# The first batch rearranged in a Strassen-type fp32 attention kernel: A's first two tiles first, x's first rows first, Wv split in A's place

## The reference

```python
# x (16, 1024, 512), adj (1024, 1024) of zeros and ones, Wq, Wk, Wv (512, 512), all float32
def _L0_gnn_ref(neuron_states, adjacency, Wq, Wk, Wv):
    q = jnp.einsum('bnd,ed->bne', neuron_states, Wq)
    k = jnp.einsum('bnd,ed->bne', neuron_states, Wk)
    v = jnp.einsum('bnd,ed->bne', neuron_states, Wv)
    rel = jnp.einsum('bnd,bmd->bnm', q, k)
    rel = adjacency.T[None, :, :] * rel
    rel = rel / jnp.linalg.norm(rel, axis=2, keepdims=True)
    return jnp.einsum('bnm,bmd->bnd', rel, v)

x = _layernorm(x + _L0_gnn_ref(x, adj, Wq, Wk, Wv), axis=-1)
```

## Time and profile before

| | us |
|---|---|
| median of 3 runs | 1971.78 (1971.39 to 1971.95) |
| the profiled execution, its own time | 1971.97 |
| its span, first to last instruction | 1970.2 |
| PE busy in the span | 1957.0 (99%) |
| DVE, ACT, POOL busy | 1531.9 (78%), 762.5 (39%), 957.8 (49%) |

### The profile page before, as it was taken

How to read it: one execution, slowest core, us unless ns; L and a number is a source line. 1 busy time by engine, 2 the same in 40 slices (tenths; PEclk the granted TensorE clock), 3 DMA queues, 4 the chain that set the end, 5 groups by cost and what they waited for, 6 DMA issues and landing times.

```text
span 1970.2 us, 28685 instructions
## 1 busy us (share of the span) xinstructions
PE 1957.0 (99%) x9857; PEld 1669.1 (85%) x9857; DVE 1531.9 (78%) x2085; ACT 762.5 (39%) x1288; POOL 957.8 (49%) x639
## 2 busy tenths in 40 slices
PE   8999999999999999999999999999999999999998
PEld 6888888888888888888888888888888888888887
DVE  8796877868778696787968779687796877868775
ACT  5433434335342352423424234342433424335341
POOL 5744536455354553446435374453644536455352
PEclk9999999999999999999999999999999999999999
DMA  5734343344524345343444333443434343344401
GB/s 188 314 134 165 144 167 115 144 154 154 186 92 149 142 157 184 122 151 118 157 175 160 128 139 133 172 153 128 160 128 170 144 155 127 144 154 152 185 26 64
DMA packets 80416, 292.22 MB, mean 148 GB/s; under 512 B 7441, under 2 KB 7441, under 8 KB 76305
## 3 DMA queue, kind: packets, MB, share of 16 engines
q1 hardware_dynamic: 80400, 292.06, 40.2%
HBM read 251.13 MB, written 40.89 MB: 148 GB/s over the span
## 4 chain that ended last, share of the span: by engine, by line
PE 97%; DVE 1%; POOL 1%; DMA 0%; issue 0%; SPq 0%; ACT 0%; POOLq 0%; DVEq 0%
PE banks L422 32%; PE banks L424 32%; PE banks L423 32%; DMA scr<-xT 0%; DVE aw L794 0%; DVE x_lo L755 0%; POOL scr L1063 0%; DVE yv L816 0%; POOL square_sum L1067 0%; POOL squares L1067 0%; SPq L344 0%; POOL scr L1072 0%; SPq L343 0%; POOL res L1075 0%; POOL res L1080 0%
## 5 line engine op out<-in xcount | busy, mean ns | idle before, releaser
L422 PE MATMUL banks<-yv 128*128 128x512 f32 x1024 | 399.8, 390 | 0.0
L424 PE MATMUL banks<-yv 128*128 128x512 f32 x1024 | 398.5, 389 | 0.0
L423 PE MATMUL banks<-yv 128*128 128x512 f32 x1024 | 398.5, 389 | 0.0
L1119 POOL TENSOR_TENSOR square_sum<-square_sum,squares 128x512 f32<-128x512 f32 x224 | 319.9, 1428 | 85.7 <-ACT squares L657 75.1
L422 PE MATMUL banks<-yv,x_hi 128*128 128x512 f32 x896 | 348.7, 389 | 0.5 <-DVE rel L857 0.5
L424 PE MATMUL banks<-yv,x_lo 128*128 128x512 f32 x896 | 348.6, 389 | 0.0
L423 PE MATMUL banks<-yv,x_hi 128*128 128x512 f32 x896 | 348.6, 389 | 0.0
L1136 POOL TENSOR_TENSOR rstd<-var_eps,minus_half 128x1 f32<-128x1 f32 x128 | 144.2, 1127 | 329.3 <-DVE var_eps L968 329.3
L423 PE MATMUL banks<-aw,x_hi 128*128 128x256 f32 x896 | 253.6, 283 | 0.0
L424 PE MATMUL banks<-aw,x_lo 128*128 128x256 f32 x896 | 253.5, 283 | 0.0
L422 PE MATMUL banks<-aw,x_hi 128*128 128x256 f32 x896 | 253.5, 283 | 0.0
(11 more groups left out here) (108 smaller groups left out, 3430.5 us busy)
## 6 DMA issues: line engine op xcount, KB each, us to landing
scr<-adj SPq DMA_DIRECT2D x128, 512.0 KB, 5.8
aw<-w_kept SPq DMA_DIRECT2D x16, 3584.0 KB, 11.1
aw<-a_kept SPq DMA_DIRECT2D x15, 3584.0 KB, 11.0
scr<-xT SPq DMA_DIRECT2D x32, 1024.0 KB, 7.1
res<-x SPq DMA_DIRECT2D x128, 256.0 KB, 2.7
out<-res SPq DMA_DIRECT2D x128, 256.0 KB, 2.0
a_kept<-aw SPq DMA_DIRECT2D x1, 3584.0 KB, 18.2
w_kept<-v_raw SPq DMA_DIRECT2D x3, 512.0 KB, 8.5
```

The costliest lines, as they stand in the source:

```text
L422: pe.matmul(bank_ap, l_hi, r_hi, start=first and i == 0, stop=False, skip_group_check=on)
L423: pe.matmul(bank_ap, l_hi, r_lo, start=False, stop=False, skip_group_check=on)
L424: mm = pe.matmul(bank_ap, l_lo, r_hi, start=False, stop=i == len(pairs) - 1, skip_group_check=on)
L1119: pool.tensor_tensor(square_sum[:, h, :], square_sum[:, h, :], squares[:, n % SQRING, :], ALU.add).then_inc(square_added, 1)
```

## The change

In the first batch:

- PE makes A in another order: k = 0, 1 for all four banks, then k = 2, 3 for banks 0 and 1, then for 2 and 3. The six idle products go.
- x's first half is loaded first; the pieces of x come in the order X11, X22, S1, X12, S2, S3, S4. S1 to S4 are all made on POOL, S1 and S2 into free space of `rel`.
- The pieces of A are ordered B11, T1, B21, T2, T4, B22, between those of x; T3's lo piece moves to POOL with a semaphore of its own.
- The staging of Wv goes: its four sums and seven lo pieces move from POOL to DVE, into the first pair of the first scores; the seven hi copies move on ACT behind the squares of m11. They write straight into `aw` once A has been stored, and the last lo piece sets `w_loaded`. The seven small stores become one of 3.5 MB, the load of Wv in the first batch goes.
- adj row 2 is loaded at the very start.

In every batch S2 stands ahead of S3. Nothing else of batches 1 to 15 changes in kind.

```diff
-X_PIECES = (X22, X11, S1, X12, S3, S2, S4)
-X_SUMS = (S1, S3, S2, S4)
+X_PIECES = (X11, X22, S1, X12, S2, S3, S4)
+X_SUMS = (S1, S2, S3, S4)
...
-        A_PIECES = (B11, T1, B21, T2, T4, T3, B22)
+        A_PIECES = (B11, T1, B21, T2, T4, B22)
...
# SP
-            load_x(0)
+            load_x(0, (0, 1))
...
+            load_adj(2)
             load_adj(3)
...
                 if first:
-                    for i in range(3, 7):
-                        store_wv(i)
-                    load_adj(2)
-                    sp.wait_ge(a_split, 7)
+                    sp.wait_ge(a_split, len(A_PIECES))
+                    sp.wait_ge(a_t3_split, 1)
                     sp.dma_start(a_kept, aw[:, :].bitcast(F32)).then_inc(a_stored, DMA)
+
+                    sp.wait_ge(w_loaded, DMA)
+                    sp.dma_start(w_kept, aw[:, :].bitcast(F32)).then_inc(w_stored, DMA)
                     for t in range(RRING):
                         load_res(0, t)
-                    for i in range(WSLOTS):
-                        sp.wait_ge(w_stored[i], 2 * DMA if i < 3 else DMA)
-                    sp.wait_ge(a_stored, DMA)
-
-                sp.wait_ge(y_done, b * Y_COUNT + Y_COUNT)
-                sp.dma_start(aw[:, :].bitcast(F32), w_kept).then_inc(w_loaded, DMA)
+                else:
+
+                    sp.wait_ge(y_done, b * Y_COUNT + Y_COUNT)
+                    sp.dma_start(aw[:, :].bitcast(F32), w_kept).then_inc(w_loaded, DMA)
                 sp.wait_ge(s_m12, b * HT + 1)
                 load_adj(6)
...
# PE
+            for ks, js in (((0, 1), range(KD)), ((2, 3), (0, 1)), ((2, 3), (2, 3))):
+                for k in ks:
+                    pe.wait_ge(w_split, 2 * k + 2)
+                    for j in js:
...
-            for i in range(FILL_PRODUCTS):
-                pe.matmul(bank[0], zeros[:, 0:P], zeros[:, 0:BANK], start=True, stop=True)
...
# ACT
+                act.wait_ge(a_stored, DMA)
+                act.wait_ge(y_done, Y_COUNT)
+                act.activation(wv_hi[:, q, :, :], wv_raw_of[q], ACT.Copy).then_inc(wv_hi_made, 1)
...
-            for q in (X22, X11, S1):
-                x_piece(0, q, True)
+            x_piece(0, X11, True)
             a_hi_piece(B11)
             act.activation(a12_raw, a_block(0, 1), ACT.Copy).then_inc(a12_copied, 1)
-            for q in (B21, B22, T1):
+            x_piece(0, X22, True)
+            a_hi_piece(T1)
+            x_piece(0, S1, True)
+            x_piece(0, X12, True)
+            for q in (B21, B22):
                 a_hi_piece(q)
-            x_piece(0, X12, True)
-            a_hi_piece(T2)
...
+                for name, i in square_order[0:2]:
+                    square(b, name, i)
                 if first:
-
-                    for i in range(WSLOTS):
-                        act.wait_ge(w_stored[i], 2 * DMA if i < 3 else DMA)
-                for name, i in square_order[0:6]:
+                    for i in range(7):
+                        wv_hi_piece(i)
+                for name, i in square_order[2:6]:
                     square(b, name, i)
...
             y_first(0)
-            x_piece(0, S3, True)
             x_piece(0, S2, True)
-            for i in range(3):
-                wv_hi_piece(i)
-            for q in (T4, T3):
+            for q in (T2, T3):
                 a_hi_piece(q)
-            x_piece(0, S4, True)
...
# DVE, start
+            x_piece(0, X11, True)
             a_lo_piece(B11)
             a_sum_of(T1)
+            x_piece(0, X22, True)
             a_lo_piece(T1)
+            x_piece(0, S1, True)
+            x_piece(0, X12, True)
+            a_lo_piece(B21)
             a_sum_of(T3)
             a_sum_of(T2)
+            x_piece(0, S2, True)
             a_lo_piece(T2)
...
# DVE, y_blocks: after y_q
                 if first:
-                    x_piece(0, S4)
+                    x_piece(b, S3, True)
+                    for j in range(2):
+                        y_lo_piece(b, B11, j, a[j])
+                    x_piece(b, S4, True)
+                    a_lo_piece(B22)
...
# DVE, s_blocks
+                if first and pair == 0:
+                    for q in WV_SUMS:
+                        wv_sum_of(q)
...
+                if first and pair == 0:
+                    wv_lo_piece(0)
+                    wv_lo_piece(1)
...
+                if first and pair == 0:
+                    wv_lo_piece(2)
+                    wv_lo_piece(3)
...
+                if first and pair == 0:
+                    for n in (4, 5, 6):
+                        wv_lo_piece(n)
...
# POOL, start
+            pool.wait_ge(x_loaded[1], DMA)
+            pool.tensor_tensor(first_raw_of[S1], x21_raw, raw_of[X22], ALU.add).then_inc(first_sum[S1], 1)
             pool.wait_ge(first_sum[S1], 1)
-            pool.wait_ge(x_loaded[0], DMA)
-            pool.wait_ge(a_split, 1)
+            pool.wait_ge(x_split, x_place[S1])
+            pool.tensor_tensor(first_raw_of[S2], first_raw_of[S1], raw_of[X11],
+                               ALU.subtract).then_inc(first_sum[S2], 1)
+            pool.wait_ge(a_hi_made, a_hi_place[T3])
+            pool.tensor_tensor(a_lo[:, T3, :, :], a_raw_of[T3], a_hi[:, T3, :, :].bitcast(F32),
+                               ALU.subtract).then_inc(a_t3_split, 1)
+            pool.wait_ge(x_split, x_place[S2])
             pool.tensor_tensor(raw_of[S3], raw_of[X11], x21_raw, ALU.subtract).then_inc(first_sum[S3], 1)
             pool.wait_ge(first_sum[S2], 1)
-            pool.wait_ge(x_split, x_place[X12])
-            pool.tensor_tensor(raw_of[S4], raw_of[X12], raw_of[S2], ALU.subtract).then_inc(first_sum[S4], 1)
+            pool.tensor_tensor(raw_of[S4], raw_of[X12], first_raw_of[S2], ALU.subtract).then_inc(first_sum[S4], 1)
```

More of the change, by code:

```diff
@@ L97, in adjacency_attention_layernorm @@
         a_stored = sem("a_stored")
-        w_stored = [sem(f"w_stored{i}") for i in range(WSLOTS)]
+        w_stored = sem("w_stored")
         a_loaded = sem("a_loaded")
@@ L196, in adjacency_attention_layernorm @@
         x_sum_place = {q: i + 1 for i, q in enumerate(X_SUMS)}
-        X_IN_TILE = {0: (X22, X11), 1: (S1,), 2: (X12,), 3: (S3,), 4: (S2,), 5: (S4,)}
+        X_IN_TILE = {0: (X11, X22), 1: (S1,), 2: (X12,), 3: (S2,), 4: (S3,), 5: (S4,)}
+        first_raw_of = dict(raw_of)
+        first_raw_of.update({S1: rel[:, 2:4, BANK:N], S2: rel[:, HT:HT + 2, 0:BANK]})
         def c11(i):
@@ L284, in wv_sum_block @@
         def wv_sum_block(i):
-            return scr[:, adj_slot[2], i * BANK:(i + 1) * BANK].rearrange("p (d e) -> p d e", d=2)
+            return v_raw[:, i, :].rearrange("p (d e) -> p d e", d=2)
         wv_raw_of = {B11: wv_block(0, 0), B21: wv_block(1, 0), B22: wv_block(1, 1),
-                     T1: wv_sum_block(0), T2: wv_sum_block(1), T3: wv_block(0, 1), T4: wv_block(1, 0)}
+                     T1: wv_sum_block(0), T2: wv_sum_block(1), T3: wv_sum_block(2), T4: wv_sum_block(3)}
         WV_PIECES = (B11, B21, B22, T1, T3, T2, T4)
         WV_SUMS = (T1, T3, T2, T4)
[L292 to L296, removed]
         def w_v(w):
@@ L315, in adjacency_attention_layernorm @@
                     T1: a_sum_block(0), T2: a_sum_block(1), T3: a_sum_block(2), T4: a_sum_block(3)}
-        A_PIECES = (B11, T1, B21, T2, T4, T3, B22)
+        A_PIECES = (B11, T1, B21, T2, T4, B22)
         A_SUMS = (T1, T3, T2, T4)
-        A_HI = (B11, B21, B22, T1, T2, T4, T3)
+        A_HI = (B11, T1, B21, B22, T2, T3, T4)
         a_place = {q: i + 1 for i, q in enumerate(A_PIECES)}
@@ L395, in batch @@
                     sp.wait_ge(v_done, b * V_COUNT + V_COUNT)
+                    if first:
+                        sp.wait_ge(a_stored, DMA)
+                        sp.wait_ge(w_stored, DMA)
                     sp.dma_start(aw[:, :].bitcast(F32), a_kept).then_inc(a_loaded, DMA)
@@ L450, in y_products @@
                     pe.wait_ge(x_split, b * 7 + x_place[left])
-                    pe.wait_ge(a_split, a_place[right])
+                    if right == T3:
+                        pe.wait_ge(a_t3_split, 1)
+                    else:
+                        pe.wait_ge(a_split, a_place[right])
                     if k == 6:
@@ L572, in x_piece @@
                     act.wait_ge(x_sum, b * 4 + x_sum_place[q])
-                act.activation(x_hi[:, q, :, :], raw_of[q], ACT.Copy).then_inc(x_hi_made, 1)
+                raw = first_raw_of[q] if first else raw_of[q]
+                act.activation(x_hi[:, q, :, :], raw, ACT.Copy).then_inc(x_hi_made, 1)
             for k in range(KD):
@@ L828, in y_blocks @@
                 a, bb, c = y_bank["a"], y_bank["b"], y_bank["c"]
-                for j in range(2):
-                    y_lo_piece(b, B11, j, a[j])
-                if first:
-                    dve.wait_ge(a_split, 7)
+                if not first:
+                    for j in range(2):
+                        y_lo_piece(b, B11, j, a[j])
                 for j in range(2):
@@ L839, in y_blocks @@
                 if first:
```

(25 more changed lines are left out.)

92 lines of the change are left out of this document (35 added, 57 removed).

## The result

| | before | after |
|---|---|---|
| median, us | 1971.74 (1971.39 to 1972.30, 6 runs) | 1979.14 (1978.83 to 1981.48, 6 runs) |
| profiled execution, us | 1971.97 | 1978.94 |
| span, us | 1970.2 | 1977.1 |
| PE busy, us | 1957.0 | 1955.7 |

The changed kernel is slower: ratio 1.0039, 95% interval 1.0026 to 1.0052. The forecast was 1978.0 and slower, in a range of 1968.5 to 1980.5.

The account below looks back on a forecast made before the run. PE was taken to bound the kernel, busy 1957.0 of 1970.2 us. The start's gain being spent, 1971.97 + 3.6 (V's round 2 late) + 2.4 (clock loss) gave 1978.0 us, range 1968.5 to 1980.5.

Parts of the forecast that it names:

- first scores start: Batch 0, end of Y: the first scores start at 40.1 to 41.0, 5.2 to 6.1 us gained.
- PE's wait for it: First pair of first scores: PE wants `s_r` at 53.8, DVE has it at 57.7; about 4 us wait.
- last Wv piece: DVE, first scores: Wv's last lo piece sets `w_loaded` at 70.6, or 67.5 with no block by POOL.
- V starts: Batch 0: V starts at 83.5, after the second pair's round 7 starts at 72.6, 1.7 us ahead.
- adj row 6 there, m22 starts: SP's queue: row 6 lands 14.1 to 15.6 us after `w_loaded`, behind the 3.5 MB store and residual tiles.
- V's round 2: V of batch 0: round 2 starts at 94.6, before 90.96, so 3.6 us late.
- PE's wait there: V of batch 0: PE is ready for round 2 at 89.3 and waits 5.3 us.
- clock lost behind it: Behind PE's wait in V: a drop to 1.2 GHz costs 2.4 us, near the earlier wait's 2.7.
- The walk: Forecast of batch 0 made by following the engines' queues piece by piece, with DVE and POOL taking turns.
- The first, a wait in V with no loss of clock: Rival: V waits but the clock stays at 2.4 GHz; 1975.6 us, chance 0.22.
- The second rival: `w_loaded` nearer 67.5, or adj rows sooner, V's round 2 at 91.5; 1970 to 1972.5 us, chance 0.22.
- The third, no collision: Rival: DVE and POOL don't collide in first scores, V's round 2 at 86.6; 1967.6 us, chance 0.13.

Follow-up runs that it names:

- PSUM operands: Changed kernel with each of Wv's four DVE sums taking its first operand from a free PSUM bank (V's values wrong); 1977.42 us, ratio to before 1.0027.
- sums late: Changed kernel with Wv's four DVE sums moved behind both `s_r` of the first pair; 1978.75 us, ratio to before 1.0036.
- The start alone: Changed kernel without Wv's sums and lo pieces (V wrong), store of Wv and residual tiles behind adj rows 6 and 7; 1966.16 us, ratio to before 0.9972.
- later last piece: Changed kernel with Wv's sums on POOL and lo pieces in the second pair, store and residual tiles still ahead of adj; 1985.61 us, ratio to before 1.0069.
- Both: Changed kernel with Wv's sums behind `s_r`, and store of Wv and residual tiles behind adj rows 6 and 7; 1971.39 us, ratio to before 0.9998.
- the first experiment: Changed kernel with the store of Wv and the four residual tiles issued behind adj rows 6 and 7; 1971.70 us, ratio to before 0.9999.
- Spread: Changed kernel with Wv's sums on POOL behind S4, lo pieces in the second pair, store and residual tiles behind adj rows; 1968.31 us, ratio to before 0.9981.
- the last version: "Spread" with POOL's T3 piece of A and its S4 held until DVE's T2 and T4 pieces are done; 1966.81 us, ratio to before 0.9974.

## Why the prediction was right, step by step

| step | forecast | measured |
|---|---|---|
| first scores start | 40.1 to 41.0 | 41.35 |
| `s_r` ready | 57.7 | 58.5 (57.89 + 0.6) |
| PE's wait for it | 4 | 3.6 |
| round 4 of the first pair | 57.9 | 58.71 |
| last Wv piece | 70.6 | 71.85 |
| V starts | 83.5 | 84.88 |
| adj row 6 there, m22 starts | 84.7 to 86.2 | 86.9 |
| V's round 2 | 94.6 | 96.39 |
| PE's wait there | 5.3 | 5.6 |
| clock lost behind it | 2.4 | 1.6 |
| sum | 1978.0 | 1978.94 profiled, 1979.14 median |

**The gain and where it went.** The walk had the right order of losses, and each link was then broken by itself: the turns of DVE and POOL (PSUM operands), SP's queue (store late), and their independence (sums late). The start alone confirms a gain of the size forecast. With the store ahead of adj, V's round 2 followed the issue of the store in four kernels: 69.84 to 95.12 (PSUM operands), 70.73 to 96.11 (sums late), 71.88 to 96.39 (changed), 76.56 to 101.65 (later last piece), so 24.5 to 25.4 us behind it.

**Terms mis-sized.** The first scores started at 41.35, outside 40.1 to 41.0: the waits in Y were near the upper ends that the walk gave, and one of 0.4 us for S1's piece, for which it had none, came ahead of them. DVE then came to Wv's sums at 47.7 and not 46.5; the six instructions took 9.1 us (47.70 to 56.76), forecast 9.4.

The time from the last piece to V's round 2 was forecast at 23.3 to 24.8 us and was 24.5; that V's round 2 came 1.8 us late is the 1.2 us of the last piece and 0.6 of this distance. Inside it, row 6 was there 15.0 us behind the last piece, in the range of 14.1 to 15.6, and from m22 to `v_p1` it took 9.4 us and not 9.0. Four residual issues took SP 4.0 us and not the 2.2 of the earlier trace rows, but the run with only them moved showed that the bytes set the landing. The last piece was late because the first scores, and DVE with them, were; in its sum 13 x 0.6 is 7.8 and not 7.9, which changes nothing.

The clock was the other way: V's round 2 to the outputs took 112.51 - 96.39 = 16.1 us against 105.46 - 90.96 = 14.5, a loss of 1.6, where I took 2.4 from the one earlier case. The two errors, + 1.8 and - 0.8, leave 1.0 in the profiled execution; that the total is so near is in part their cancelling. By the medians the change is 7.4 us, forecast 6.0.

PE's wait in V came out at 5.6 for 5.3 also because both its ends were late, V's start by 1.4 and round 2 by 1.8. And V's start had another cause than forecast: no wait for the second pair's `s_u2`, but slow matmuls behind the wait for `s_r`.

**The first clock loss was absorbed.** PE's stretch behind the wait for `s_r` in the changed kernel shows 1.2 GHz, as does the end of the wait in V (columns as in the stretch of "Both"):

```profile
60.00:62.00 2.00, 2.00 (x6) 0.50 0.04 8
...
94.00:96.30 2.30, 0.00 (x0) 0.50 1.04 400
```

From round 4 of the first pair to V it took 84.88 - 58.71 = 26.2 us, before 85.21 - 60.68 = 24.5. That 1.6 us cost nothing, because V's round 2 wasn't waiting for PE. The prediction said so of such a drop.

**The rivals.** The first, a wait in V with no loss of clock, is not what the profiled execution shows: the clock was at 0.50 when PE resumed. The second rival, gain just given back, is what the first experiment measured once the store was out of the way (1971.7); in the changed kernel the last piece came at 71.85, not near 67.5, and adj did not overtake the store. The third, no collision, needed work left out or moved. Batches 1 to 15 were costed at nothing: no wait of PE after V's round 2, and 277.16 - 156.15 = 121.01 us a batch against 270.10 - 149.10 = 121.00.

## What to carry to other kernels

In a queue that only issues DMAs a large transfer delays everything written behind it, needed or not. Before adding one, list what stands behind it and put what somebody waits for ahead. A wait in such a queue does the same when it ends later than what the entries behind it need: here it cost next to nothing in the changed kernel, and 12 us (64.6 to 76.6) when the last piece of Wv came later than m12. Work moved to an engine with idle time must be priced in the stretch where it lands and by its operands: here a 0.6 us instruction cost up to 1.7 where VectorE read two operands from SBUF while GpSimd worked on SBUF too. When one late resource sets a stage's end, gains in front of it don't count: taking away a 3.6 us wait gained 0.4 us with the store ahead, and 0.3 with it behind, where other waits took its place, while moving the store and the residual tiles gave 7.4 us with one edit.

## What the runs showed of the hardware

Which waits of PE bring its clock to 1.2 GHz was less regular than I took it. Waits of 3.0 to 6.6 us brought it in every profiled execution here, at a cost of about 1.6 us each in the changed kernel and its edits, where the 4.2 us wait before had cost 2.7; 16.3 us cost 2.6 (118.70 - 101.65 against 14.5). A wait of 2.0 us brought it in the kernel with both edits and not in the one with the sums late, at the same place. The two 2 us waits in Y left it at 2.4 GHz in the changed kernel and brought it down in three others with the same Y (PSUM operands, the start alone, "Spread"), where the second of them was followed by 9.9 us to the first scores and not 8.3. This spread of 1 to 2 us may be what separates executions of one kernel: of the seven of the start alone the two longest (1967.35 and 1967.96) have the lowest mean clock, 0.998, and the others (1965.87 to 1966.25) 0.999 or 1.000. In the last version no such order is seen (1967.99 at 1.000), so it stays open.
